# A two-model block on one core: the first model's early batches placed among the second model's weight preparation, in one written order

## What is computed

```python
# L0, per batch
h = layernorm(x) * (1 + g1) + be1                    # g1, be1, a1, ... = [t, c] @ Wc + bc
x = x + a1 * softmax(h @ Wq @ (h @ Wk).T / 16) @ (h @ Wv)
h = layernorm(x) * (1 + g2) + be2
x = x + a2 * gelu(gelu(h @ W1 + b1) @ W2 + b2)       # 256 -> 1024 -> 256
# L1: _weight_quant of every weight
scale = 1.0 / clip(mean(abs(w)), 1e-05)
w_quantised = clip(round(w * scale), -1, 1) / scale
# L1, conditioning network, once for the 16 rows
h = bitlinear(silu(c), wa0)
h = bitlinear(silu(gate) * y, wa2)                   # gate, y = split(bitlinear(h, wa1))
params = bitlinear(rmsnorm(bitlinear(h, wa3) + ba3), wa4) + ba4     # wa4 is 1536 x 1536
# L1, per batch
mx = layernorm(x) * (1 + sc) + s
i, f, g = bitlinear(mx, wi), sigmoid(bitlinear(mx, wf)), bitlinear(mx, wg)
o = scan(silu(i) * (1 - f), f)
x = x + g_msa * bitlinear(rmsnorm(o) * silu(g), wo)
x = x + g_mlp * bitlinear(silu(gate) * y, wm2)       # gate, y = split(bitlinear(my, wm1)), 256 -> 2048
```

## Time and profile before

| what | value |
|---|---|
| median of three runs | 789.7 us |
| the profiled execution: its time / its span | 789.95 us / 788.1 us |
| TensorE busy | 628.5 us, 80% |
| VectorE busy | 620.6 us, 79% |
| ScalarE busy | 568.3 us, 72% |
| GpSimd busy | 458.3 us, 58% |
| mean granted TensorE clock | 0.912 |

### The profile page before, as it was taken

One profiled execution on the slowest core, in us unless ns is written; L12 is line 12 of the kernel. 1 busy time (PEld: TensorE's weight loads), 2 busy tenths in 40 slices (PEclk: granted clock), 3 DMA queues, 4 the chain that ended last, 5 costly groups with the idle time before them and its releaser, 6 DMA issues.

```text
span 788.1 us, 13091 instructions
## 1 busy us (share of the span) xinstructions
PE 628.5 (80%) x3560; PEld 487.7 (62%) x3588; DVE 620.6 (79%) x1432; ACT 568.3 (72%) x1206; POOL 458.3 (58%) x647
## 2 busy tenths in 40 slices
PE   0631336899899999999999999999999998874552
PEld 0110212678777878888787878788888877642321
DVE  3779888223768999999899989998899889888653
ACT  1234670447689999898989999998989888774431
POOL 2203360213647686867767686867678586856623
PEclk9955579799999999999999999999999999985866
DMA  8495800111010101202021011112021010110100
GB/s 312 150 408 204 297 0 25 30 38 47 1 68 35 46 37 48 68 15 68 13 67 47 33 47 47 37 43 66 14 67 34 22 40 22 49 34 1 34 14 14
DMA packets 17821, 51.96 MB, mean 66 GB/s; under 512 B 2880, under 2 KB 3712, under 8 KB 16880
## 3 DMA queue, kind: packets, MB, share of 16 engines
q1 hardware_dynamic: 17488, 50.92, 18.7%
q10 hardware_dynamic: 288, 0.52, 0.2%
HBM read 47.10 MB, written 4.33 MB: 65 GB/s over the span
## 4 chain that ended last, share of the span: by engine, by line
PE 58%; DVE 20%; issue 9%; POOL 5%; ACT 5%; DMA 2%; SPq 1%; DVEq 0%; POOLq 0%; ACTq 0%
PE bank L1346 15%; PE bank L1401 14%; PE bank L1339 7%; PE bank L1474 6%; PE bank L1326 5%; PE bank L1392 5%; DVE qa_dx L872 4%; PE bank L1318 2%; PE bank L1524 2%; PE bank L1489 2%; DVE arena L1138 2%; DVE qa_am L860 2%; DMA arena<-wo_dram 1%; POOL arena L512 1%; DVE arena L1009 1%
## 5 line engine op out<-in xcount | busy, mean ns | idle before, releaser
L1392 PE MATMUL bank<-arena,w 128*128 128x256 f32 x512 | 117.8, 379 | 0.0
L1401 PE MATMUL bank<-arena,w 128*128 128x256 f32 x512 | 116.7, 381 | 1.0 <-ACT arena L633 1.0
L1392 PEld LDWEIGHTS bank<-arena,w 128*128 128x128 f32 x512 | 96.1, 190 | 15.0
L1401 PEld LDWEIGHTS bank<-arena,w 128*128 128x128 f32 x512 | 94.9, 190 | 13.0 <-ACT arena L633 1.2
L1326 PE MATMUL bank<-ident,arena 128*128 128x128 f32 x448 | 66.9, 283 | 21.8 <-ACT arena L685 16.1
L1474 PE MATMUL bank<-tern_wm,qTm 128*128 128x512 bf16 x228 | 71.5, 403 | 15.1 <-ACT arena L707 6.2
L512 POOL TENSOR_TENSOR arena<-arena,row_nm 128x1024 f32<-128x1024 f32 x32 | 75.4, 2357 | 6.6 <-ACT junk_u L715 6.6
L1326 PEld LDWEIGHTS bank<-ident,arena 128*128 128x128 f32 x448 | 53.1, 145 | 35.1 <-issue 20.1
L694 ACT ACTIVATE arena<-arena,round_col,qa_qs 128x256 f32<-128x256 f32 x96 | 50.5, 592 | 22.4 <-DVE qa_qs L881 22.4
L1346 PE MATMUL bank<-arena 128*128 128x256 f32 x256 | 61.5, 383 | 3.1 <-DVE arena L899 3.1
L827 DVE BATCH_NORM_STATS2 ln_st<-arena 128x6 f32<-128x256 f32 x128 | 48.0, 417 | 18.1 <-POOL arena L502 11.7
(11 more groups left out here) (212 smaller groups left out, 1729.2 us busy)
## 6 DMA issues: line engine op xcount, KB each, us to landing
arena<-rows_d SPq DMA_DIRECT2D x32, 384.0 KB, 3.8
arena<-wa_dram SPq DMA_DIRECT2D x12, 768.0 KB, 10.0
arena<-x_dram SPq DMA_DIRECT2D x16, 256.0 KB, 2.6
arena<-rows_d SPq DMA_DIRECT2D x16, 256.0 KB, 3.4
out_dram<-arena SPq DMA_DIRECT2D x16, 256.0 KB, 2.0
arena<-Wc_dram SPq DMA_DIRECT2D x1, 3072.0 KB, 14.5
arena<-wm_dram SPq DMA_DIRECT2D x1, 2048.0 KB, 7.6
w<-W_dram SPq DMA_DIRECT2D x2, 1024.0 KB, 9.1
```

What stands on the lines that cost most here:

```text
L1392: last = te.matmul(bank[3 - q % 2][:, m * S:(m + 1) * S], w1[:, k, (2 * q + m) * P:(2 * q + m + 1) * P], h2T[:, k, :], start=k == 0, stop= ...
L1401: last = te.matmul(bank[3][:, c * S:(c + 1) * S], w2[:, k, c * P:(c + 1) * P], g[:, k, :], start=k == 0, stop=k == HC - 1)
```

## The change

`SCHEDULE`, `EARLY` and the loop are gone. One string, `ORDER`, names every part with its batch, weights' parts included, and each engine walks it once and takes what is its own. It begins:

```diff
+ORDER = """
+load_cond0 load_x:0 load_cond1 load_qkv load_g0 ada_c ada0_sq ada0_z vec2 ada0_r cond_mm0 vec3 ln1_moments:0 ada0_q
+ln1_rstd:0 ln1_norm:0 cond_f0 xn1T:0 hT:0 cond_mm1 rows0_turned cond_f1 k_mm:0 rows0_copy store_rows0 q_mm:0 kT:0 abs_wa0
+abs_wa1 load_rows0:0 load_x:1 qT:0 load_rows0:1 load_mlp load_g1 s_mm:0 v_mm:0 xb:0 score_max:0 load_x:2 ln1_moments:1
...
+def run_pipeline(eng, parts, order):
...
+    for entry in order.split():
+        name, _, i = entry.partition(":")
+        if name in parts:
+            parts[name](Batch(int(i or 0)))
```

In it L0's batches 0 and 1 stand wholly, batch 2 up to its last turn and batch 3 up to its attention ahead of the last part of the conditioning network (`ada5_y`); of L1 only batch 0's `ln3_moments` and `ln3_rstd` stand ahead of it. The last part of L0's batch 15 (`x3:15`) stands just behind `gate_u:11`. To hold the results, `x3` becomes a ring of eight buffers, and L0 may be up to eight batches ahead:

```diff
+RING = 8
...
-                wait(dve, s["x4_ready"], b.back(2))
-                ve.tensor_tensor(x3[b.p], halves(2), x2[b.p], ALU.add).then_inc(s["x3_ready"], 1)
+                wait(dve, s["x4_ready"], b.back(RING))
+                ve.tensor_tensor(x3[b.i % RING], halves(2), x2[b.p], ALU.add).then_inc(s["x3_ready"], 1)
```

The five weights that are used once (wa0, wa1, wa2, wa3 and wa4) are no longer rounded. VectorE makes two matrices of 0 and 1 straight from float32, "above 0.5" and "below -0.5", and TensorE adds the product with the first and the negated rows' product with the second:

```diff
+                    ve.tensor_scalar(out, place, winv[:, j:j + 1], 0.5, ALU.mult, ALU.is_gt).then_inc(s["wclip"], 1)
...
+                    ve.tensor_scalar(below, place, winv[:, j:j + 1], -0.5, ALU.mult, ALU.is_lt).then_inc(s["wtern"], 1)
...
+                            te.matmul(out, aqT[:, k * NB:(k + 1) * NB], AW[name][:, cols], start=k == 0, stop=False)
+                            last = te.matmul(out, minus_aqT[:, k * NB:(k + 1) * NB], BELOW[name][:, cols], start=False,
+                                             stop=k == K // P - 1)
```

```diff
+        BY_DVE = ["wa1", "wm1", "a6"]
+        BY_ACT = ["wa0", "wa2", "wa3", "wi", "wf", "wg", "wo", "wm2"] + [f"a{i}" for i in range(KC4) if f"a{i}" not in BY_DVE]
...
+        ROUND_POOL = ["wi", "wf", "wg", "wo", "wm2"]
+        ROUND_ACT = ["wm1"]
```

L0's condition is computed with features on partitions at once, 48 products of a 128 x 128 piece of `Wc` with 16 columns, in two halves, and `Wc` is loaded in two halves, ahead of everything else:

```diff
+                    for m in range(3 * C * h, 3 * C * (h + 1)):
+                        for k in range(4):
+                            last = te.matmul(bank[5 - h][:, m * NB:(m + 1) * NB], wc[:, k, m * P:(m + 1) * P], tcT[:, k * NB:(k + 1) * NB],
+                                             start=k == 0, stop=k == 3)
```

More of the change, by code:

```diff
@@ L51, in wait @@
[L51 removed]
+    if value > 0:
+        eng.wait_ge(sem, value)
 def wait_dma(eng, sems, b):
     value = (b.i - b.p) * 8 + 16
[L57 to L82 removed]
+    if value > 0:
+        eng.wait_ge(sems[b.p], value)
@@ L178, in build_program @@
         y2T = take2(0, C, S)
[L179 to L184 removed]
+        x2 = [take2(0, T, D) for _ in range(2)]
+        X3_AT = used[0]
+        x3 = [take2(0, T, D) for _ in range(RING)]
         small = {}
@@ L551, in _ @@
+            for n in range(len(LAYERS)):
+                parts[f"ada{n}_r"] = ada_rstd(n)
+            for n in ROUND_POOL:
+                parts[f"round_{n}"] = rounded(n)
+            walk(pool, parts)
         @block.scalar
@@ L593, in part, with silu_hidden, evac_h @@
+            def silu_hidden(_):
+                act.wait_ge(s["ada_mm"], 2)
+                for k in range(2):
+                    last = sc.activation(hz[:, k * 448:(k + 1) * 448], bank[6 + k][0:NB, 0:448], ACT.Silu,
+                                         scale=QN["a"]["dq"][0:NB, 0, 0:1])
+                last.then_inc(s["ada_gate"], 1)
+            def evac_h(bk_, scale, shift, modulated, out, mm, ready, *free):
                 def part(b):
+                    if b.i == 0:
+                        act.wait_ge(s["cond_steps"], modulated)
+                        act.wait_ge(s["feat_loaded"], 96)
@@ L1305, in _ @@
+            for n in (0, 1, 2, 3, 5):
+                parts[f"ada{n}_z"], parts[f"ada{n}_q"], parts[f"ada{n}_qT"] = ada_weighted(n), ada_quant(n), ada_evac(n)
+            for k in range(len(GROUPS) + 1):
+                parts[f"mean{k}"] = means(k)
+            for n in BY_DVE:
+                parts[f"abs_{n}"] = absum_of(n)
+            for n in TERNARY_ORDER + [f"b{k}" for k in range(KC4)]:
+                parts[f"tern_{n}"] = ternary(n)
             walk(dve, parts)
```

1145 lines of the change are left out of this document (631 added, 514 removed), and 11 rows, old and new, of the table SCHEDULE.

## The result

The changed kernel takes **800.8 us** (median of four runs, 799.7 to 801.2) beside 790.0 us for the kernel before (four runs): a ratio of 1.0135, with a 95% interval from 1.0115 to 1.0155. It is 1.35% slower, where 10.9% faster was forecast.

The account below looks back on a forecast made before the run. TensorE was taken to bound the middle, with 35.0 us of work per batch. Terms 168 + 450 + 84 gave 702 us of span, plus 1.85 a time of 704 us, 10.9% below; range 676 to 748.

Parts of the forecast that it names:

- Term 1: Start until `ada5_y` ends, the conditioning network with early first-model batches on TensorE: 168 us, from 150 to 185.
- the chain at 200: Rival, 17%: the network's linked steps wait behind first-model pieces; `ada5_y` ends at 200 to 212, time 738 to 750.
- the low clock: Rival, 3%: TensorE's clock stays at the lower level up to `ada5_y`, which ends at 260 or later; 798 or more.
- 1.2 times: Second passes over weight chunks on VectorE: the trace's means for float32 against bf16, 1058 against 860 ns.
- Term 2: From `ada5_y` to `x3` of batch 15: 450 us, set by TensorE's work of 443, at 95% or more busy.
- 1.016: Factor on TensorE's work behind `ada5_y`, from before's written-out steps: 35.57 us for 35.0 of work.
- the middle leaks: Rival, 6%: an order without a period can't keep TensorE and VectorE nearly full; at 93% the time is 731.
- Term 3: The drain behind `x3` of batch 15, with 68 us of second-model VectorE work left: 84 us, from 76 to 95.
- The upper bound of 109 us: The drain if VectorE did its 68 us of work at before's rate, 63%.
- The sign: Whole kernel against before: faster 96%, same 1%, slower 3%.
- the rival with 3%: Slower kernel, 3%: TensorE's clock stays at the lower level up to `ada5_y`; time 798 us or more.

Follow-up runs that it names:

- e1: Changed kernel, but behind the conditioning network in the kernel before's step order, first model two steps further ahead: 788.4 us, 0.997 of before.
- e2: Order of e1, but the two steps without first-model work lie in the middle instead of at the end: 787.1 us, 0.9957 of before.
- e7: Order of e1, but the second model's first two steps carry no first-model work, later ones are those of before: 780.05 us, 0.9885 of before.
- e17: Order of e7 with GpSimd's long passes cut to a quarter of their columns, the rest uncomputed: 759.1 us, 0.9618 of before.
- e16: Changed kernel with GpSimd's long passes cut to a quarter of their columns, the rest uncomputed: 767.6 us, 0.9713 of before.

## Why the prediction was wrong

- **Term 1 (`ada5_y` at 168 us) came out**: 172.2, in part by luck. TensorE was busy for 142.81 us (129 forecast) and idle for 29 (39 forecast), so two misses of 10 and more us nearly cancel. The clock was 0.96. No rival of this term came: not the chain at 200, not the low clock. The second passes over a chunk cost 1.01 us each, as taken from L1138. But 860 ns for the old second pass L1140 was a mean over meetings, which the prediction's comparison "1.2 times" didn't see. Before's timeline has such a pass beside GpSimd's rounding and one without it:

```profile
110.69 4.91 POOL L414 TENSOR_SCALAR arena<-arena,winv 128x1536 f32<-128x1536 f32 x2
114.31 1.71 DVE L1140 TENSOR_SCALAR arena<-arena 128x1536 bf16<-128x1536 bf16 x1
116.91 0.56 DVE L1140 TENSOR_SCALAR arena<-arena 128x1536 bf16<-128x1536 bf16 x1
```

Nine of the twelve took 0.56 us, three 1.7 to 1.8; of L1138, eleven took 0.94 to 0.96 and one 2.25. Alone they stand 1.7 to one, close to the 1.8 that the prediction set beside them. G stood in the rows of before.

- **Term 2 (450 us to `x3:15`) is the step that failed**: it took 516 (688.6 less 172.2). It priced the stretch by TensorE's total, 443 us x 1.016, "at 95% or more". TensorE did 461.7 us (the four windows' sum), 19 more than forecast, at 89%. Some 55 us are idle time, and the 1.016 stood for a repeated step. The sentence that "an order that isn't a repeated step may well leave gaps" had the cause (e1 shows it: the same parts in repeated steps go at 98%), and the rival *the middle leaks* its 6%, but even that rival's 93% was too much: four batches went at 91%, four at 84%.
- **What the term left out** shows in e1, e2 and e7, which have no leak. L1's 16 batches must pass through a pipeline of four lagged steps that can't start ahead of `ada5_y`. Filling it took 93 us in the best order tried and emptying it 85.5; between them stand 12 batches, for which L0's absence is worth 2.4 us each (35.7 to 33.3), since L1's own chain through VectorE, ScalarE, GpSimd and TensorE took 33 us a batch though VectorE works only 27 in it. GpSimd's long passes are 4 us of that (e17), the rest isn't split. So the 80 us of L0 work ahead of `ada5_y` could give back only what filled the start before: 47 us (140.3 to 92.9), for 37 that it costs there. The forecast sum asked for 534 us behind `ada5_y` (450 + 84); e7 needs 605.
- **Term 3 (the drain in 84 us) failed the same way**: 110.3 us, with 75.8 us of VectorE work (68 forecast) at 69%. That its parts are "packed by what is ready" assumed that batches of L1 can overlap up to VectorE's full work. L1 alone runs at 33 us per batch in e1, with VectorE at 82%, and the last batch has nothing beside it. The upper bound of 109 us, by the 63% of before, lay next to the result, but by luck: its work was 8 us too little and its rate too low.
- **The cost of an order**: meetings of VectorE and GpSimd weren't among the terms or the rivals, though before has 37 us of them in its own rows; in after they come to 39 us more. How much of the lost time they cause isn't shown: e16 against e17 gives 12 us with GpSimd's own time in it, and 8 for the rest.
- **The sign**: the rival with 3% had the clock as its mechanism, which stayed at 0.96. The kernel is slower by another way: 38 paid, 41 back, 22 lost in the middle, 8 gained at the end. A mechanism for a slow middle ended at 731 only because the gain of terms 2 and 3 was taken as certain. (The rivals' times stand some 2 us above their own terms, 200 + 450 + 84 + 1.85 being 736 and not 738, which decides nothing.)

## What to carry to other kernels

Filling idle time ahead of a second stage paid here only as much as that stage's own pipeline got shorter: measure first what the second stage takes per batch with nothing beside it (here 33 us, for 35.7 with everything), since that and not the bound engine's total prices the work that is moved away. Where the middle runs at 97% of one engine, keep its repeated step and put the change around it; a free order must be shown to hold the pace, and one engine's work total doesn't show that. Look at who runs beside whom: a small VectorE pass on SBUF beside a wide GpSimd pass can take several times its time, and a mean over such passes hides it.

## What was unexpected of the hardware

- VectorE and GpSimd: a pass of 160 ns (`qo_dx`, 128 x 2) takes 1005 ns more when it starts beside a GpSimd pass; passes with one operand in PSUM and reduces don't wait (3 ns), and none waits beside a GpSimd pass over 128 x 2. GpSimd at 766 ns for 128 x 256, 1312 for 128 x 512 and 2369 for 128 x 1024 sets both the length of a meeting and the price of cutting it.
- An L1 step alone ran at a granted clock of 0.62 to 0.70, with TensorE busy for 55% of it in short bursts between waits.
- Writing out the loop changed the time by 0.09%, inside its interval.
